# The first batch of an attention and expert kernel, written out by itself: keys ahead of queries, in pairs, partly with fp32 operands

## The chip, the core and the metric

The kernel runs on one core of one Trainium2 chip. The metric is the device time of one execution in microseconds (us); three runs of the kernel before are given, and one further execution that the profiler recorded. TensorE (PE) does matrix products, VectorE (DVE) and ScalarE (ACT) elementwise work, GpSimd (POOL) spreads rows over partitions, and SyncE (SP) issues the DMAs. Each engine works through its own queue in order and waits on semaphores of the others.

## What is computed

```python
x = L0_attn_x                       # (8, 1024, 256), 8 batches
x = _layernorm(x + _L0_attn_ref(x, L0_attn_Wqkv, L0_attn_bqkv, L0_attn_Wln, L0_attn_bln), axis=-1)
x = _layernorm(x + _L0_ffn_ref(x, L0_ffn_expert_sel, L0_ffn_keys, L0_ffn_values), axis=-1)

# attention, with b batches, N = 1024 rows, C = 256
qkv = x @ Wqkv + bqkv
q, k, v = jnp.split(qkv, 3, axis=2)
q = q - q.mean(axis=2, keepdims=True)
k = k - k.mean(axis=2, keepdims=True)
q2 = q * q
k2 = k * k
q2 = q2 / (q2.sum(axis=2, keepdims=True) + EPS_SUM)
q2 = _l2norm(q2, axis=-1)
k2 = k2 / (k2.sum(axis=2, keepdims=True) + EPS_SUM)
k2 = _l2norm(k2, axis=-2)
kv = jnp.einsum('bnc,bnd->bcd', k2, v)
t2 = jnp.einsum('bnc,bcd->bnd', q2, kv) / math.sqrt(N)
return (v + t2) @ Wln + bln

# 16 experts of width 128
sel = jax.nn.sigmoid(jnp.einsum('bsd,ed->bse', input_tensor, expert_sel))
scores = jax.nn.relu(jnp.einsum('bsd,edh->bseh', input_tensor, keys))
out = jnp.einsum('bseh,ehv,bse->bsv', scores, values, sel)
```

## The kernel before

A batch has 8 tiles of 128 rows (T = 8), in two groups of four. Nearly every fp32 product is made of three fp32r products: each operand is split into a high part, which ScalarE copies in fp32r, and a low part, which VectorE (in one place GpSimd) makes as the difference. `product` (L966 to L975) issues high times high, high times low and low times high.

The stages of layer 1 carry short names. QK projects one tile to q and k (512 columns). GG adds one tile's part to G = x^T k2, which stands for k2^T x. KS sums the columns of k2 and k2^2 over all tiles with products of 2 columns. KV makes G times Wv Wln. QT transposes two tiles of q2, Y makes the attention output of one tile from x times Wv Wln and q2 times kv, XT transposes the normalised tile x1, LG makes the expert logits of one group. ZA and ZN are the end of layer 2. Layer 2 runs in steps: in step s of an iteration TensorE makes the up product of one expert for one group, VectorE gates it (relu times sel, L950), ScalarE and VectorE split the gated tile (`gated_h`, `gated_l`), and TensorE makes the down product one step later. An iteration has 32 steps; the table LOOP says which stages of the batch ahead are done in which step, so that layer 1 of batch b + 1 lies under layer 2 of batch b.

Layer 1 of the first batch has nothing to lie under. The kernel before runs an iteration number -1 for it with the same step function, without the expert products, after the table FIRST: steps 7 to 14 with one QK each and GG behind, then KS, KV, QT 0 and 1, Y 0 to 3, XT 0 to 3 and LG 0. Tiles 4 to 7 of QT and Y stay for iteration 0. Odd tiles of QK use other buffers (`up_bank` and `gated` instead of `qk_bank` and `qk`), so names of layer 2 turn up in rows of layer 1. `wqk_split_hi` and `wqk_split_lo` centre and split the projection weights, `centre_qk_bias`, `spread_bv`, `make_wvl` (L981 to L992) and `wvl_esel_hi`, `wvl_esel_lo` prepare bias, Wv Wln and the selection weights. GpSimd makes the low part of the second half of xT and adds the fourth powers of k (`k4_total`, L474).

The expert weights come in eight pieces, alternating keys and values. `weights_hi` and `weights_lo` (L927) split them at the steps of PIECE_STEPS and PIECE_LO_STEPS, three in iteration -1 and five in iteration 0. The function table for the sigmoid is loaded at step 20 of iteration -1 (L651), before the logits are copied.

## Time and profile before

| | |
|---|---|
| runs | 1044.91, 1043.44, 1042.62 us, median 1043.44 |
| profiled execution, its own time | 1041.46 us |
| its span, first to last instruction | 1039.6 us |
| busy: TensorE, VectorE, ScalarE, GpSimd | 1008.7, 796.1, 509.2, 219.9 us |
| mean granted TensorE clock | 0.995 of full |
| chain that ended last | TensorE 95%, VectorE 3%, ScalarE 1% |

The busy times are those of the instructions' own records, which overlap a little on each engine: a product of 256 columns has a record of 0.28 us, and the next starts 0.11 to 0.12 us after it. How long a row of instructions takes is therefore best read from the chain that ended last, where each piece lasts until the next one begins. The idle time of an engine counts only where another waits for it.

### The profile page before, as it was taken

To read this page: it belongs to the slowest core of one execution; us is meant where nothing else is said; L and a number is where in the kernel's file an instruction comes from. 1 tells how busy PE (TensorE), PEld (TensorE's weight loads), DVE (VectorE), ACT (ScalarE), POOL (GpSimd) and SP (SyncE) were. 2 spreads that over 40 slices of the span, in tenths; PEclk is the share of its full clock that TensorE was granted. 3 is DMA by queue.
4 is the path that set the end of the run, shared out by engine and by line. 5 is a ranking of instruction groups with operands and counts; after the bars stand their busy time and mean duration, and the time that the engine had idled before them with its cause. 6 is when DMAs were issued, how large, how long until landed. Compare 5 with 4: busy or idle time off the path is not lost.

```text
span 1039.6 us, 18353 instructions
## 1 busy us (share of the span) xinstructions
PE 1008.7 (97%) x6636; PEld 914.7 (88%) x6636; DVE 796.1 (77%) x1818; ACT 509.2 (49%) x1192; POOL 219.9 (21%) x273
## 2 busy tenths in 40 slices
PE   5789999999999999999999999999999999999997
PEld 4669899988999899998999989999899988999986
DVE  6888886878868787778877779687886878867565
ACT  6555643465434653356534565255653465434332
POOL 2121122211221121221212211221122211221221
PEclk9999999999999999999999999999999999999999
DMA  5032000200011000110001100011000200000000
GB/s 180 21 117 68 2 22 1 83 21 3 21 43 62 2 2 21 43 61 2 2 21 43 61 3 21 1 57 48 2 22 1 83 21 3 22 2 21 2 21 21
DMA packets 12122, 32.59 MB, mean 31 GB/s; under 512 B 1792, under 2 KB 2048, under 8 KB 12032
## 3 DMA queue, kind: packets, MB, share of 16 engines
q1 hardware_dynamic: 12032, 31.42, 8.9%
q8 instruction: 53, 0.87, 0.3%
q14 instruction: 37, 0.30, 0.1%
HBM read 22.50 MB, written 8.39 MB: 30 GB/s over the span
## 4 chain that ended last, share of the span: by engine, by line
PE 95%; DVE 3%; ACT 1%; issue 0%; DMA 0%; ACTq 0%
PE down_bank L974 34%; PE up_bank L974 34%; PE ring_bank L974 10%; PE qk_bank L974 8%; PE g_bank L974 4%; PE ring_bank L1073 1%; PE ring_bank L1057 1%; PE ring_bank L1083 1%; PE ring_bank L1082 1%; PE ring_bank L1038 1%; DMA x<-in_wqk 0%; DVE keys_l L927 0%; DVE k_l L870 0%; DVE qk L738 0%; DVE q L922 0%
## 5 line engine op out<-in xcount | busy, mean ns | idle before, releaser
L504 ACT ACTIVATE gated_h<-gated 128x512 fp32r<-128x512 f32 x256 | 161.4, 631 | 403.4 <-DVE gated L950 403.4
L490 POOL PARTITION_BROADCAST sel_all<-sel_rows x240 | 196.8, 820 | 710.6 <-DVE gated L950 709.9
L974 PE MATMUL down_bank<-vals_h,gated_h 128*128 128x256 f32 x1024 | 292.0, 285 | 0.9 <-DVE gated_l L956 0.8
L974 PE MATMUL down_bank<-vals_l,gated_h 128*128 128x256 f32 x1024 | 285.3, 279 | 0.0
L974 PE MATMUL down_bank<-vals_h,gated_l 128*128 128x256 f32 x1024 | 285.3, 279 | 0.0
L950 DVE SCALAR_TENSOR_TENSOR gated<-up_bank,sel_all 128x512 f32<-128x512 f32 x256 | 176.0, 688 | 63.2 <-PE up_bank L974 62.0
L956 DVE TENSOR_TENSOR gated_l<-gated,gated_h 128x512 fp32r<-128x512 f32 x256 | 173.3, 677 | 43.5 <-ACT gated_h L504 42.5
L974 PE MATMUL up_bank<-x1T_h,keys_l 128*128 128x512 f32 x512 | 202.3, 395 | 0.0
L974 PE MATMUL up_bank<-x1T_l,keys_h 128*128 128x512 f32 x512 | 202.0, 394 | 0.0
L974 PE MATMUL up_bank<-x1T_h,keys_h 128*128 128x512 f32 x512 | 201.3, 393 | 0.0
L974 PEld LDWEIGHTS down_bank<-vals_h,gated_h 128*128 128x128 f32 x1024 | 193.2, 189 | 9.1 <-DVE gated_l L956 3.2
L974 PEld LDWEIGHTS down_bank<-vals_l,gated_h 128*128 128x128 f32 x1024 | 192.9, 188 | 4.6
L974 PEld LDWEIGHTS down_bank<-vals_h,gated_l 128*128 128x128 f32 x1024 | 192.7, 188 | 0.0
L974 PEld LDWEIGHTS up_bank<-x1T_h,keys_l 128*128 128x128 f32 x512 | 96.7, 189 | 20.4
L974 PEld LDWEIGHTS up_bank<-x1T_l,keys_h 128*128 128x128 f32 x512 | 96.9, 189 | 11.5
L974 PEld LDWEIGHTS up_bank<-x1T_h,keys_h 128*128 128x128 f32 x512 | 96.7, 189 | 11.1
L738 DVE TENSOR_TENSOR qk<-qk_bank,qk_bias 128x512 f32<-128x512 f32 x60 | 41.3, 689 | 36.6 <-PE qk_bank L974 36.6
L974 PE MATMUL qk_bank<-wqk_h,xT_h 128*128 128x512 f32 x120 | 50.0, 417 | 9.8 <-DVE xT_l L718 9.8
L751 DVE TENSOR_TENSOR y<-ring_bank,x_raw 128x256 f32<-128x256 f32 x64 | 27.0, 423 | 31.3 <-PE ring_bank L974 31.3
L974 PE MATMUL qk_bank<-wqk_h,xT_l 128*128 128x512 f32 x120 | 48.3, 402 | 0.0
L974 PE MATMUL qk_bank<-wqk_l,xT_h 128*128 128x512 f32 x120 | 48.3, 402 | 0.0
L504 ACT ACTIVATE k_h<-k,k_scale 128x256 fp32r<-128x256 f32 x64 | 32.6, 509 | 28.1 <-DVE k_scale L785 27.5
(156 smaller groups left out, 1655.1 us busy)
## 6 DMA issues: line engine op xcount, KB each, us to landing
xT_raw<-in_xT SPq DMA_DIRECT2D x16, 512.0 KB, 3.7
x_raw<-in_x SPq DMA_DIRECT2D x16, 512.0 KB, 4.5
out<-z SPq DMA_DIRECT2D x32, 256.0 KB, 2.3
w_room<-in_keys SPq DMA_DIRECT2D x4, 512.0 KB, 4.7
z<-in_values SPq DMA_DIRECT2D x4, 512.0 KB, 3.8
sel_rows<-sel SPq DMA_DIRECT2D x64, 8.0 KB
x<-in_wqk SPq DMA_DIRECT2D x1, 512.0 KB, 3.5
sel_all<-in_b_qk SPq DMA_DIRECT2D x1, 256.0 KB, 5.6
```

What stands on the lines that cost most here:

```text
L490: nc.gpsimd.partition_broadcast(sel_all[:, e % 2], row, P).then_inc(sel_spread, 1)
L504: return nc.scalar.activation(dst, src, ACT.Copy, **kw)
L738: V.tensor_tensor(qk_of(it, t)[:], qk_bank_of(it, t)[:], qk_bias[:], ALU.add).then_inc(qk_biased, 1)
L751: V.tensor_tensor(y[:, a % 2], ring_of(it, s, "Y", a)[:, 0:C], x_raw[:, a], ALU.add).then_inc(y_added, 1)
L950: V.scalar_tensor_tensor(out=gated[:], in0=up_bank[s % 2][:], scalar=0.0, in1=sel_all[:, s % 2], op0=ALU.max, op1=ALU.mult).then_inc(gate_ ...
L956: V.tensor_tensor(gated_l[:, s % 2], gated[:], gated_h[:, s % 2].bitcast(F32), ALU.subtract).then_inc(gated_lo, 1)
L974: last = mm(dst, lhs, rhs, start=start and i == 0, stop=stop and i == n - 1, **kw)
L1038: last = mm(bk[:, j:j + 2], total[:, m * P:(m + 1) * P], ones[:, 0:2], start=True, stop=True)
L1057: last = nc.tensor.transpose(bk[:, j:j + P], q2[:, 2 * a + i, m * P:(m + 1) * P], ident[:])
L1073: last = nc.tensor.transpose(bk[:, m * P:(m + 1) * P], x1[:, a, m * P:(m + 1) * P], ident[:])
L1082: mm(bk[:], esel_hl[:, m], x1T_h[:, a, m], start=(m == 0), stop=False)
L1083: last = mm(bk[:], esel_h[:, m], x1T_l[:, a, m], start=False, stop=(m == M - 1))
```

## The change

The iteration -1 is gone. Each engine has a function `first_batch`, which it runs before the loop and in which its part of the first batch is written out in its own order.

- TensorE projects the keys alone, two tiles at a time into one bank (`qk0`, `keys0`), with the bias as a last product of a row of ones and a split bias (`bias_hl`); queries follow in pairs later (`queries0`), pairs 2 and 3 only around the transposes of x1. Squares are taken by ScalarE straight from the bank.
- G, KV and the q part of Y are plain fp32 products (`g0`, `kv0`, `y0_of_q`): x, the normalised k2, G and kv are not split for them. The x part of Y (`y0_of_x`) stays in three fp32r products and is issued ahead of the column sums and KV.
- The sums over tiles of k2 and k2^2 are kept for even and odd tiles apart, both on VectorE, and the column sums have eight products instead of four. GpSimd has no elementwise work any more.
- wqk is loaded and treated in its key half and its query half, and the first batch's xT in four quarters.
- Two weight pieces instead of three are split before the loop, six in the loop. In iteration 0 the stages QT 2, QT 3 and Y 4 come one step later (FIRST_PLAN).
- In all batches q_sum and the floor that was made from it are gone; a constant floor Q_FLOOR^2 is applied to the sum of fourth powers (`lift_q4`), and ScalarE's two other activations on q keep or drop their accumulated sum accordingly.

The core of the diff, first the tables and the loads, then ScalarE, VectorE and TensorE. Functions named there and not shown do what their line in the list above says, with one wait for what they read and one for the buffer that they write.

```diff
+FIRST_PLAN = {
+    0: [], 1: [("QT", 2)], 2: [("QT", 3)], 3: [("Y", 4)], 4: [("Y", 5)], 5: [("Y", 6), ("XT", 4)],
+    6: [("Y", 7), ("XT", 5)]}
+FIRST = dict(LOOP, plan={**LOOP["plan"], **FIRST_PLAN})
...
-SIGMOID_STEP = 20
-PIECE_STEPS = ((-1, 9), (-1, 17), (-1, 20), (0, 0), (0, 2), (0, 3), (0, 5), (0, 7))
-PIECE_LO_STEPS = ((-1, 10), (-1, 18), (-1, 21), (0, 1), (0, 3), (0, 4), (0, 6), (0, 8))
-PIECE_LOADS = ((-1, 11), (-1, 19), (-1, 24), (0, 1), (0, 3), (0, 4))
+EARLY_PIECES = 2
+PIECE_STEPS = ((0, 0), (0, 1), (0, 4), (0, 6), (0, 8), (0, 10))
+PIECE_LO_STEPS = ((0, 1), (0, 2), (0, 5), (0, 7), (0, 9), (0, 11))
+PIECE_LOADS = ((0, 1), (0, 2), (0, 4), (0, 6), (0, 8))
+QUARTER = GN // 2
...
+            def load_xT0(p):
+                cols = slice((p % 2) * QUARTER, (p % 2 + 1) * QUARTER)
+                at_least(sp, xT0_lo, p - 1)
+                sp.dma_start(xT_raw[:, :, cols], xT[0, :, p // 2, :, cols]).then_inc(xT0_in[p], 16)
+            sp.dma_start(wqk_raw[:, :, 1], wqk[:, :, 1]).then_inc(w_k_in, 16)
+            load_xT0(0)
             sp.dma_start(bqk_raw, b_qk.partition_broadcast(P)).then_inc(bias_in, 16)
+            load_xT0(1)
...
+            for p in (2, 3):
+                load_xT0(p)
+            sp.dma_start(x_raw[:, GT:T], x_dram[0, :, GT:T]).then_inc(x_in[1], 16)
             for i in range(2):
                 load_piece(i)
+            sp.wait_ge(piece_lo, 1)
+            load_piece(2)
+            move_rows(0, 0, 0)
             def step(it, s):
...
+                        nc.scalar.activation(k0[:, i], k0_bank(p)[:, i * C:(i + 1) * C], square,
+                                             accum_out=k_sum[:, i:i + 1]).then_inc(k0_squared, 1)
+                def k_fourths(p):
+                    act.wait_ge(k0_normed, p + 1)
+                    at_least(act, k0_fourth_summed, p - 1)
...
+                        t = 2 * p + i
+                        nc.scalar.activation(q2[:, t], q0_bank(p)[:, i * C:(i + 1) * C],
+                                             square).then_inc(q0_squared, 1)
+                    for i in range(2):
+                        t = 2 * p + i
+                        act.wait_ge(q0_squared, t + 1)
+                        nc.scalar.activation(q0_bank(p)[:, i * C:(i + 1) * C], q2[:, t], square,
+                                             accum_out=q4_sum[:, t:t + 1]).then_inc(q0_fourth, 1)
...
+                act.wait_ge(constants_set, 2)
+                nc.scalar.activation(table_ahead[:, 0:1], eps_ln[:], sqrt)
+                w_hi(1, 1)
+                xT_pair_hi(0)
+                act.wait_ge(qk_bias_set, 2)
+                copy(bias_hl, qk_bias[:], scale=2.0 / P).then_inc(bias_hi, 1)
+                xT_pair_hi(1)
+                k_squares(0)
+                w_hi(0, 2)
+                k_fourths(0)
+                k_squares(1)
+                xT_pair_hi(2)
+                k_fourths(1)
+                k_squares(2)
+                xT_pair_hi(3)
+                act.wait_ge(wvl_made, 1)
+                copy(wvl_h[:].rearrange("p m c -> p (m c)"), down_bank[0][:]).then_inc(wvl_hi, 1)
+                copy(wvl_f.rearrange("p m c -> p (m c)"), down_bank[0][:]).then_inc(wvl_copied, 1)
+                k_fourths(2)
+                k_squares(3)
+                k_fourths(3)
+                q_squares(0)
+                act.wait_ge(g0_made, T)
+                copy(gated[:], g_bank[:]).then_inc(g0_copied, 1)
+                q_squares(1)
+                act.wait_ge(cols0_copied, 1)
+                nc.scalar.activation(col_norm[:], col_sums[:, 0:M], sqrt).then_inc(cols0_rooted, 1)
+                act.wait_ge(q0_lifted, 1)
+                nc.scalar.activation(q_root[:, 0:GT], q4_lifted[:, 0:GT], sqrt).then_inc(q0_rooted, 1)
+                act.wait_ge(constants_set, 5)
+                act.wait_ge(small_in, 64)
+                copy(esel_hl[:, :, 0:E], esel_raw[:])
+                copy(esel_h[:, :, 0:E], esel_raw[:]).then_inc(esel_hi, 1)
+                for p in range(2):
+                    act.wait_ge(q0_transposed, p + 1)
+                    copy(qT0[p].rearrange("p i m n -> p (i m n)"), q0T_bank(p)[:]).then_inc(q0_copied, 1)
+                weights_hi(0)
+                for p in range(2):
+                    for a in (2 * p, 2 * p + 1):
+                        act.wait_ge(y_aggregated, tile(0, a))
+                        nc.scalar.activation(y_std[:, a % 2:a % 2 + 1], y_mv[:, a % 2, 1:2], sqrt,
+                                             bias=eps_ln[:]).then_inc(y_rooted, 1)
+                    if p == 0:
+                        for m in range(M):
+                            act.wait_ge(kv0_scaled, m + 1)
+                            copy(kvw_h[:, m], kvw0[:, m]).then_inc(kv_hi, 1)
+                    for a in (2 * p, 2 * p + 1):
+                        act.wait_ge(x1_transposed, tile(0, a))
+                        copy(x1T_h[:, 0, :, a * P:(a + 1) * P],
+                             y0_bank(a)[:, 0:C].rearrange("p (m n) -> p m n", m=M)).then_inc(x1T_hi, 1)
+                q_squares(2)
+                q_squares(3)
+                act.wait_ge(q0_lifted, 2)
+                nc.scalar.activation(q_root[:, GT:T], q4_lifted[:, GT:T], sqrt).then_inc(q0_rooted, 1)
+                nc.scalar.activation(table_ahead[:, 1:2], eps_ln[:], ACT.Sigmoid)
+                act.wait_ge(logits_made, 1)
+                copy(sel[:], logits0_bank[LOW:LOW + E, :]).then_inc(logits_low, 1)
...
+                def k_normalised(p):
+                    dve.wait_ge(k0_squared, 2 * p + 2)
+                    V.tensor_scalar(k_sum_eps[:], k_sum[:], EPS_SUM, None, ALU.add).then_inc(k0_eps, 1)
+                    dve.wait_ge(k0_eps, p + 1)
+                    V.reciprocal(k_scale[:], k_sum_eps[:]).then_inc(k0_scaled, 1)
+                    dve.wait_ge(k0_scaled, p + 1)
+                    at_least(dve, g0_made, 2 * (p - 1))
+                    at_least(dve, k0_fourth, p - 1)
+                    V.tensor_tensor(k0_normal[p % 2], k0[:], k_scale[:].unsqueeze(2).broadcast_to((P, 2, C)),
+                                    ALU.mult).then_inc(k0_normed, 1)
...
+                w_centre(1, 1, w_k_in)
+                w_lo(1, 1)
+                xT_pair_lo(0)
+                qk_bias_centred()
+                bias_rows()
+                xT_pair_lo(1)
+                spread_bv()
+                k_normalised(0)
+                w_centre(0, 2, w_q_in)
+                xT_pair_lo(2)
+                k_normalised(1)
+                k_total(1)
+                w_lo(0, 2)
+                xT_pair_lo(3)
+                k_normalised(2)
+                k_fourth_total(1)
+                k_total(2)
...
+                k_normalised(3)
+                k_fourth_total(2)
+                k_total(3)
+                k_fourth_total(3)
...
+                x_bias(0)
...
+                q_lift(0)
+                q_scales(0)
...
+                for m in range(M):
...
+                x_bias(1)
+                for a in range(2):
+                    y_add(a)
+                for a in range(2):
+                    y_finish(a)
+                for a in range(2):
+                    y_add(2 + a)
+                    x1T_low(a)
+                for a in range(2):
+                    y_finish(2 + a)
+                weights_lo(0)
+                for a in range(2):
+                    x1T_low(2 + a)
...
+                q_lift(1)
+                dve.wait_ge(logits_low, 1)
+                V.tensor_tensor(sel[:], logits0_bank[0:E, :], sel[:], ALU.add).then_inc(logits_summed, 1)
+                q_scales(1)
+                for i in range(2):
+                    x_bias(2 + i)
+                weights_lo(1)
...
+            def first_batch():
+                def qk0(bank, p, a):
+                    cols = slice(a * C, (a + 1) * C)
+                    for i in range(2):
+                        h, n = divmod(2 * p + i, GT)
+                        product(bank[:, i * C:(i + 1) * C],
+                                [(both(xT_h, xT_l, ALL, h, m, slice(n * P, (n + 1) * P)),
+                                  both(wqk_h, wqk_l, ALL, m, cols)) for m in range(M)],
+                                start=i == 0, stop=False, skip_group_check=True)
+                    pe.wait_ge(constants_set, 5)
+                    pe.wait_ge(bias_lo, 1)
+                    return mm(bank[:], ones_r, bias_hl[:, cols].unsqueeze(1).broadcast_to((P, 2, C)),
+                              start=False, stop=True, skip_group_check=True)
...
+                def g0(p):
+                    pe.wait_ge(k0_normed, p + 1)
+                    pe.wait_ge(x_in[p // 2], 16)
+                    for i in range(2):
+                        a = 2 * p + i
+                        for m in range(M):
+                            last = mm(g_bank[:, m * C:(m + 1) * C], x_raw[:, a, m * P:(m + 1) * P],
+                                      k0_normal[p % 2][:, i], start=(a == 0 and m == 0), stop=(a == T - 1),
+                                      skip_group_check=True)
...
+                            last = nc.tensor.transpose(q0T_bank(p)[:, j:j + P], q2[:, 2 * p + i, m * P:(m + 1) * P],
+                                                       ident[:])
+                    last.then_inc(q0_transposed, 1)
+                def y0_of_q(a):
+                    pe.wait_ge(q0_copied, a // 2 + 1)
+                    pe.wait_ge(kv0_scaled, M)
...
+                keys0(0)
+                keys0(1)
+                make_wvl()
+                g0(0)
+                keys0(2)
+                g0(1)
+                keys0(3)
+                g0(2)
+                make_bvl()
+                queries0(0)
+                g0(3)
+                queries0(1)
+                y0_of_x(0)
+                y0_of_x(1)
+                column_sums()
+                kv0()
+                y0_of_x(2)
+                y0_of_x(3)
+                q0_transpose(0)
+                q0_transpose(1)
+                for a in range(GT):
+                    y0_of_q(a)
+                queries0(2)
+                for a in range(GT):
+                    x1_transpose(a)
+                    if a == 1:
+                        queries0(3)
+                logits0()
```

On VectorE, at the start, the kernel before has this (names without buffer numbers; `x` is the room in which wqk is staged):

```order
L670 TENSOR_REDUCE minus_mean<-x 128x4
L672 TENSOR_SCALAR minus_mean<-minus_mean 128x4
L676 SCALAR_TENSOR_TENSOR wqk_l<-x,minus_mean,wqk_h 128x256 x4
L718 TENSOR_TENSOR xT_l<-xT_raw,xT_h 128x1024
L682 TENSOR_REDUCE bias_mean<-sel_all 128x2
L684 TENSOR_SCALAR bias_mean<-bias_mean 128x2
L687 TENSOR_SCALAR qk_bias<-sel_all,bias_mean 128x256 x2
L696 TENSOR_SCALAR y<-ones,bv_col 128x128 x2
```

The changed kernel has this in the same place:

```order
L975 TENSOR_REDUCE minus_mean<-x 128x2
L977 TENSOR_SCALAR minus_mean<-minus_mean 128x2
L986 SCALAR_TENSOR_TENSOR wqk_l<-x,minus_mean,wqk_h 128x256 x2
L994 TENSOR_TENSOR xT_l<-xT_raw,xT_h 128x2x256
L999 TENSOR_REDUCE bias_mean<-sel_all 128x2
L1001 TENSOR_SCALAR bias_mean<-bias_mean 128x2
L1004 TENSOR_SCALAR qk_bias<-sel_all,bias_mean 128x256 x2
L1012 SCALAR_TENSOR_TENSOR x1T_h<-qk_bias,x1T_h 64x512
L994 TENSOR_TENSOR xT_l<-xT_raw,xT_h 128x2x256
L1020 TENSOR_SCALAR y<-ones,bv_col 128x128 x2
```

The same steps stand in the same order at half the width, with the bias rows (L1012) and a second quarter of xT put in.

On ScalarE, at the end of the prologue, up to the first split of a gated tile, before:

```order
L504 ACTIVATE x1T_h<-ring_bank 128x2x128 x2
L651 ACT_TABLE_LOAD
L651 ACTIVATE table_ahead<-eps_ln 128x1
L504 ACTIVATE keys_h<-w_room 128x1024
L504 ACTIVATE sel<-ring_bank 16x512
L573 ACTIVATE sel<-sel 16x512
L504 ACTIVATE gated_h<-gated 128x512
```

And in the changed kernel, from the last squares of the queries (`q` and `q_sum` are order's short names for q2 and q4_sum):

```order
L662 ACTIVATE g_bank,q_sum<-q 128x256 x2
L657 ACTIVATE q<-down_bank 128x256 x2
L662 ACTIVATE down_bank,q_sum<-q 128x256 x2
L718 ACTIVATE q_root<-q_lifted 128x4
L719 ACT_TABLE_LOAD
L719 ACTIVATE table_ahead<-eps_ln 128x1
L494 ACTIVATE sel<-down_bank 16x512
L723 ACTIVATE sel<-sel 16x512
L494 ACTIVATE vals_h<-z 128x1024
L494 ACTIVATE gated_h<-gated 128x512
```

Two pairs of queries and a root now stand ahead of the table load, and the weight piece stands behind the sigmoid.

On VectorE, between the sum of the logits and the first two gates, before:

```order
L909 TENSOR_TENSOR sel<-ring_bank,sel 16x512
L927 TENSOR_TENSOR keys_l<-w_room,keys_h 128x1024
L922 TENSOR_SCALAR q<-q,q_scale 128x256 x4
L950 SCALAR_TENSOR_TENSOR gated<-up_bank,sel_all 128x512
L956 TENSOR_TENSOR gated_l<-gated,gated_h 128x512
```

And in the changed kernel:

```order
L1165 TENSOR_TENSOR sel<-down_bank,sel 16x512
L1053 RECIPROCAL q_scale<-q_root 128x4
L1057 TENSOR_SCALAR q<-q,q_scale 128x256 x4
L1064 TENSOR_TENSOR x_raw<-x_raw,out_bias 128x512 x2
L947 TENSOR_TENSOR vals_l<-z,vals_h 128x1024
L960 SCALAR_TENSOR_TENSOR gated<-up_bank,sel_all 128x512
L966 TENSOR_TENSOR gated_l<-gated,gated_h 128x512
```

A reciprocal and two additions of the bias to x have come in ahead of the first gate.

## Rows read from the trace of the kernel before

**Rows 1.** Stretches: start:end, us, busy time of each engine, clock, DMA share, GB/s.

```profile
0.00:9.80 9.80, 0.00 (x0) 0.03 (x1) 4.43 (x8) 4.76 (x8) 0.93 (x8) 1.00 0.81 257
9.80:64.59 54.79, 41.46 (x216) 33.44 (x216) 44.67 (x113) 32.30 (x96) 11.55 (x12) 0.94 0.19 62
64.59:100.00 35.41, 35.41 (x238) 32.46 (x238) 30.71 (x63) 20.61 (x43) 7.36 (x9) 1.00 0.35 117
```

**Rows 2.** Waits of TensorE, whole span: us in total, times, longest.

```profile
PE g_bank L974 <- DVE k_l L870: 6.3, 4, 2.6
...
PE down_bank L974 <- DVE gated_l L956: 0.8, 1, 0.8
```

**Rows 3.** Chain that ended last, the start: start us, us, what.

```profile
0.72 3.54 DMA x<-in_wqk
...
4.29 1.23 DVE minus_mean L670
...
5.75 1.70 ACT wqk_h L510 x4
...
8.43 1.24 DVE xT_l L718
...
9.80 2.90 PE qk_bank L974 x6
```

**Rows 4.** DMA issues by line: count, KB each, median us from issue to landing.

```profile
out<-z SPq DMA_DIRECT2D x32, 256.0 KB, 2.3
...
ident<-in_ident SPq DMA_DIRECT2D x1, 64.0 KB, 5.1
```

**Rows 5.** Timeline, the prologue: start us, us, engine, line, operation.

```profile
5.81 0.85 SPq L426 DMA_DIRECT2D ident<-in_ident  x1
...
39.78 0.99 PE L1038 MATMUL ring_bank<-ones,k_total 128*128 128x2 f32 x8
```

**Rows 6.** Chain that ended last, pieces used as prices.

```profile
14.11 1.73 PE down_bank L987 x8
...
16.70 1.42 PE qk_bank L974 x6
...
26.15 1.13 DVE keys_l L927
27.29 0.60 DVE qk L738
...
34.69 0.40 ACT qk L554 x2
...
64.18 0.44 PE ring_bank L1057 x4
...
69.10 1.36 PE down_bank L974 x12
```

**Rows 7.** Timeline, end of the prologue.

```profile
56.05 1.28 ACT L651 ACT_TABLE_LOAD   x1
...
57.34 0.20 ACT L651 ACTIVATE table_ahead<-eps_ln 128x1 f32<-128x1 f32 x1
...
58.51 0.59 ACT L504 ACTIVATE sel<-ring_bank 16x512 f32<-16x512 f32 x1
...
59.13 0.68 DVE L909 TENSOR_TENSOR sel<-ring_bank,sel 16x512 f32<-16x512 f32 x1 [2.04 <-ACT sel L504]
...
60.87 1.67 DVE L922 TENSOR_SCALAR q<-q,q_scale 128x256 f32<-128x256 f32 x4
...
62.47 0.67 DVE L950 SCALAR_TENSOR_TENSOR gated<-up_bank,sel_all 128x512 f32<-128x512 f32 x1
...
64.59 0.39 PE L974 MATMUL down_bank<-vals_h,gated_h 128*128 128x256 f32 x1
```

**Rows 8.** Timeline, step 2 of the loop.

```profile
70.41 0.66 DVE L956 TENSOR_TENSOR gated_l<-gated,gated_h 128x512 fp32r<-128x512 f32 x1
...
71.67 0.28 PE L974 MATMUL down_bank<-vals_h,gated_h 128*128 128x256 f32 x1
```

647 lines of the change are left out of this document (388 added, 259 removed), and 5 rows, old and new, of the table plan.

## The prediction

> **What bounds the kernel now.** Read the stretches first [rows 1]. In the first 9.80 us TensorE does nothing, in the next 54.79 us it is busy for 41.46, and from 64.59 us, where the first product with the values of an expert starts, it is busy without a gap (35.41 of 35.41 us, and so on to the tail). From there the kernel is a TensorE queue of fixed length, and the change leaves that part's products as they are. So only one number matters: the moment at which that first down product starts, plus what is left of TensorE's work behind it. The waits [rows 2] say what holds it before: the key products of G wait 6.3 us in all for the low parts that VectorE makes, and the first down product waits for VectorE too (0.8 us). The prologue is therefore a relay of VectorE, ScalarE and TensorE, with TensorE filling what it can. The sum is made against the profiled execution: span 1039.6 us, its own time 1041.46 us; the median of the runs is 1043.44 us, 2.0 above it, and I forecast the median by taking the difference off it.
>
> **The start.** The chain [rows 3] is: 3.54 us for the 512 KB of wqk, then a reduction of 1.23, ScalarE's four high parts 1.70, xT high, xT low 1.24, first product at 9.80. The change loads and treats only the key half of wqk and a quarter of xT first. 256 KB land in 2.3 us for an output pair, against 3.54 for the 512 KB [rows 3, 4]; I take 2.5, landing at 3.2 (bounds 3.0 and 4.3). Everything behind is half as wide: reduction 0.7, scaling 0.2, two high parts 0.9, xT high 0.6, xT low 0.7 make the first product start at 6.4, which is 3.4 earlier. The first products still run at the half clock: six of 512 columns took 2.90 us right after the idle start and 1.42 later [rows 3, 6]. Half the columns twice over is the same work, so the first pair ends near 9.5; its closing bias product waits for the bias chain on VectorE, which ends near 9.1.
>
> **The key rounds.** VectorE's queue now holds the spread of b_v ahead of the first k_normalised, and that needs the small loads. The last of them was issued at 5.81 and landed 5.1 later, at 10.9 [rows 4, 5]; 256 KB less stand ahead of it, at 257 GB/s [rows 1] that is 1.0 us, so about 10.1. Behind it, in handed-over steps, priced at 0.60 to 0.7 for 512 columns on VectorE, 0.40 for a square of 256 on ScalarE [rows 6]: spread 0.5, normalising pair 0 1.1 (to 11.65), centring the query half 0.8 (12.4), its high parts 0.9 and the fourth powers 0.5 on ScalarE (13.8), squares of pair 1 0.85 (14.65), xT high and low of quarter 2 1.35 (16.0). TensorE meanwhile did pair 1, wvl and G of pair 0, to 14.9, and waits 1.1. Then pair 2 to 17.8, its squares to 18.6, xT high and low of quarter 3 to 20.0.
>
> **TensorE's stretch.** From 20.0 it has its own queue to do, and VectorE keeps ahead of it: four wvl products in fp32 took 1.73 us, 0.43 each, against three fp32r products of 256 columns at 0.113 each (twelve in 1.36) [rows 6]. So fp32 costs TensorE 0.09 us per product more, and saves the splitting into high and low parts on the two engines that are waited for. The list is keys pair 3 1.6, G 1.7, bvl 0.85, queries 1.6, G 1.7, queries 1.6, two x parts of Y 1.4, and eight column sums. Eight records, which are four such products, took 0.99 [rows 5], so eight take 1.7 to 2.0. Sum 12.3, to 32.3. KV in fp32 and two more x parts (3.1) lie beside VectorE's work on the column sums, bias on x, q scales and kv: 0.3, 0.6, 0.7 with two square roots of ScalarE, 1.5, 1.6, to 37.1. That is when the q part of Y can start. Four q parts in fp32 take 3.45, queries pair 2 1.6. VectorE's add, statistics and normalisation of each of tiles 0 to 3 are three instructions of 256 columns, the price of a square (0.40), with short ones between, 1.5 a tile; in one queue with two low parts of x1T they end near 45.6, transposing and ScalarE's last high part at 46.4.
>
> **The tail of the prologue,** where the change puts work that was not there before. ScalarE now squares queries of pairs 2 and 3 (eight at 0.40, 3.3), takes a root (0.35 with VectorE's lift), loads the sigmoid table (1.28) and only then copies the logits (0.60) [rows 6, 7]. The table load lay beside the logits products before and costs its full length now. That makes 52.0, the sum on VectorE (0.68) 52.7. Behind that sum VectorE has four scalings of q (0.2 for the reciprocal, 1.6 as in the row of four), two biases on x (1.2), and a weight piece (1.13) before the first gate: 56.8. GpSimd's spread of sel lies beside it. Before, one piece and the four scalings stood there. From gate to down product 62.47 to 64.59, 2.1 us [rows 7]. The down product thus starts at 58.9; some fifteen hand-overs of 0.03 to 0.05 that I rounded away add 0.4: **59.3, against 64.59, a gain of 5.3**.
>
> What is given back: at that moment QT 3 was already done before and is not now, four transposes, 0.4 [rows 6]. TensorE will have stood for about 6 us between the second up product and this down product with only a few transposes in it. The clock was at its lower level after 9.8 idle us until the first six products had run, which cost 2.90 - 1.42 = 1.5 [rows 3, 6]; I take 1.5 again (bounds 0 and 2.0). Six weight pieces are split within the first batch's loop instead of five, at steps 1, 2, 5, 7, 9, 11 instead of 1, 3, 4, 6, 8. A piece is 1.13 of VectorE. The tightest place that I saw is step 2, where gated_l (70.41, 0.66 long) ended 0.6 ahead of its product at 71.67 [rows 8]; the Y that made it tight moves to step 3 with the extra piece, others have 1 to 2.9, and only step 12 gets a piece that is not compensated. I count 0.3. Sum: -5.3 + 0.4 + 1.5 + 0.3 = -3.1. The removal of q_sum, its floor and its maximum, and of the accumulate for every tile lies on engines that nobody waits for later, nothing. 1043.44 - 3.1 = **1040.4 us**.
>
> **The rivals.**
> A, the clock does not fall or the wait is short, 0.18: the 1.5 is not paid, -4.6, 1038.8. For it: the transposes in the gap; against: the gap is about 6 us long, and the only gap of that size before the loop was followed by the low clock.
> B, the start does not come early, 0.20: four loads are cut into runs half as long. If these halves landed at half the rate, about 1 MB would need 3.7 us more before the query half and quarter 2 arrive, and VectorE waits for these from 11.6 on. The down product starts at 62.6 and the sum is +0.2: 1043.6, no change. For it: the DMA engines are at 0.81 of their time in the first stretch [rows 1]; against, the packets are no smaller than 1 KB.
> C, slower, 0.09: the six pieces in the first twelve steps. VectorE is busy 30.71 of 35.41 us there [rows 1]. With one more piece and Y shifted, each piece that is not covered stops TensorE for 1.13 at the down product of that step. It decides from the third on, since 3 x 1.13 = 3.4 is more than the 3.1 won; with five of six, 5.6 less the 0.3 counted, the sum is +2.2: 1045.6. Against: the slack of 1 to 2.9 at the other steps.
> D, the table load holds ScalarE longer than its row, 0.05: a second 1.28 on the path, -1.8, 1041.6. In the trace the load runs 56.05 to 57.33 and the next activation starts at 57.34 [rows 7], which speaks against it.
> The Trainium skill, "ScalarE: Activation LUTs", section "What ACT_TABLE_LOAD costs", puts a drain of about 1380 ns beside the load of 1283 ns; the load agrees with the row, the drain is not seen in it. By that rule the time would be 1041.8 us, since the load is now on the path; by the row it is 1040.4.
> E, more is won, 0.08: the relay rows are shorter than handed-over ones wherever two steps follow on one engine (0.60 instead of 0.69), over some thirty such steps 2.5 more, 1037.9.
> The forecast itself has 0.40.
>
> **How the numbers follow.** About 0.2%, 2.1 us, is what a measurement of this kernel can tell from no change. The forecast lies 1.0 beyond that, and its own spread (w_k landing 3.0 to 4.3, column sums 1.7 to 2.0, clock 0 to 2.0) is about 2 either side: 0.30 of its 0.40 is faster, 0.10 the same. A and E are faster (0.26), with 0.05 of B: 0.61. Same: 0.10, 0.14 of B, 0.04 of D: 0.28. Slower: C, 0.01 of B and 0.01 of D: 0.11. The range takes in E, A and B and leaves out C and the far end of E: 1036.3 to 1044.9.
>
> **What would show it.** First product at 6.4 (wrong if after 8: rival B), fourth key pair at about 20, then TensorE gapless for 12 us; q part of Y at 37; VectorE behind ScalarE's table load and not the logits products as what releases sel; first down product at 59.3; its twelve matmuls at 0.21 apart if the clock is low, 0.113 if not (A); no wait of TensorE on gated_l afterwards (C). The prediction is wrong in its main step if the down product starts before 57 or after 61.5.

## The result, and the profile after

The kernel after takes **1053.9 us** (median; five runs lie from 1052.6 to 1054.2, and a sixth, of 1446.85 at a granted clock of 0.654, is left out), the kernel before 1044.2 (six runs, 1042.6 to 1047.1). The ratio is 1.0083, with a 95% interval of 1.0066 to 1.0101: slower by 0.8%, 9.7 us, where the forecast was 1040.4 and the range ended at 1044.9. The profiled execution took 1054.15 us, its span is 1052.4.

The first lines of the page after (us, share of the span, count):

```profile
span 1052.4 us, 18293 instructions
...
PE 1028.3 (98%) x6672; PEld 934.5 (89%) x6672; DVE 785.5 (75%) x1782; ACT 498.2 (47%) x1117; POOL 211.7 (20%) x266
```

TensorE is busy for 98% of the span, before for 97%. But that is 1028.3 us with 6672 product records, and the kernel before, with the same loop, is busy for 1008.7 with 6636. The stretches, to hold against [rows 1] (start:end, us, busy time with counts, clock, DMA share, GB/s):

```profile
core 0: us, PE busy (x) PEld busy (x) DVE busy (x) ACT busy (x) POOL busy (x), PEclk, DMA share, GB/s
0.00:9.80 9.80, 2.58 (x12) 2.61 (x12) 3.66 (x9) 2.91 (x5) 1.33 (x10) 1.00 0.69 191
9.80:62.81 53.01, 43.83 (x238) 37.89 (x238) 34.31 (x88) 26.85 (x78) 2.77 (x3) 0.92 0.25 78
62.81:100.00 37.19, 37.19 (x236) 34.10 (x237) 30.23 (x62) 20.51 (x42) 7.36 (x9) 0.94 0.32 108
...
300.00:900.00 600.00, 600.00 (x3926) 546.15 (x3925) 464.84 (x1059) 297.34 (x672) 125.80 (x153) 1.00 0.08 27
```

The first down product starts at 62.81, before at 64.59: the prologue is 1.8 us shorter, where 5.3 were forecast. From there to the end of the span are 989.6 us, before 975.1: **14.5 us more in the part that the prediction had taken as fixed.** TensorE hardly stands still there: its one listed wait is of 0.7 us, behind 1000 us, and the kernel before has one of 0.8 in the same place. In the 600 us from 300 to 900, in which TensorE is fully busy in both kernels, the view after counts 3926 products, and that of the kernel before 3975:

```profile
300.00:900.00 600.00, 600.00 (x3975) 546.48 (x3974) 471.67 (x1087) 304.63 (x721) 126.70 (x155) 1.00 0.08 28
```

So the same products follow each other more slowly. A stretch of the chain of work that ended last (start us, us, what), after, and then the same of the kernel before:

```profile
482.74 1.44 PE down_bank L1185 x12
484.18 1.40 PE up_bank L1185 x6
...
486.97 1.42 PE down_bank L1185 x12
488.39 1.40 PE up_bank L1185 x6
...
491.90 1.42 PE down_bank L1185 x12
```

```profile
481.27 1.38 PE down_bank L974 x12
482.65 1.37 PE up_bank L974 x6
...
489.60 1.42 PE down_bank L974 x12
491.01 1.40 PE up_bank L974 x6
...
493.81 1.38 PE down_bank L974 x12
495.19 1.37 PE up_bank L974 x6
```

Twelve down products take 1.42 to 1.44 here, and mostly 1.36 to 1.39, at times 1.42, before. Worked out from the starts of the products in the traces between 100 and 1000 us (means, gaps over 150 and 300 ns left out): one down product follows the other after 119.0 ns, before after 115.8, and one up product after 232.2, before after 230.4. In 256 steps of twelve and six that is 9.8 and 2.8 us, 12.6 of the 14.5. (By e1 below, whose 64 bytes alone take 11.9 off this part, 2.6 are left.) The rest was forecast in kind: 0.4 for QT 3 and 1.5 for the low clock, of which more below.

The waits of TensorE after, to hold against [rows 2]:

```profile
PE qk_bank L1185 <- DVE xT_l L994: 7.2, 1, 7.2
PE down_bank L1185 <- DVE gated_l L966: 5.1, 2, 4.4
PE down_bank L1314 <- DVE x1T_l L1087: 1.5, 1, 1.5
PE qk_bank L1206 <- DVE x1T_h L1012: 1.4, 1, 1.4
```

The waits of G's products for the low parts of the keys, 6.3 us before, are gone, as meant. The first down product waits 4.4 us for gated_l. The other 0.7 of that row, and the whole row of 0.8 in [rows 2], lie behind 1000 us: before, the first down product has no wait for gated_l in the list.

### The profile page after: what moved, and what is told of

The parts are those of the page before. It is cut to its first block, busy times and chain, and to the rows that moved or that the text cites. A ratio compares the mean times of both kernels' runs of the same rounds, so it can differ in the third digit from the quotient of the medians.

```text
span 1052.4 us, 18293 instructions
## 1 busy us (share of the span) xinstructions
PE 1028.3 (98%) x6672; PEld 934.5 (89%) x6672; DVE 785.5 (75%) x1782; ACT 498.2 (47%) x1117; POOL 211.7 (20%) x266
## 4 chain that ended last, share of the span: by engine, by line
PE 96%; DVE 2%; ACT 1%; DMA 1%; issue 0%; SPq 0%; DVEq 0%
PE down_bank L1185 35%; PE up_bank L1185 34%; PE ring_bank L1185 9%; PE qk_bank L1185 8%; PE g_bank L1185 4%; PE ring_bank L1418 1%; PE ring_bank L1402 1%; PE g_bank L1229 1%; PE ring_bank L1425 1%; PE ring_bank L1424 1%; DMA sel_all<-in_b_qk 1%; PE ring_bank L1387 1%; DVE q L1057 0%; PE down_bank L1239 0%; PE ring_bank L1298 0%
## 5 line engine op out<-in xcount | busy, mean ns | idle before, releaser
L1185 PE MATMUL down_bank<-vals_h,gated_l 128*128 128x256 f32 x1024 | 289.5, 283 | 0.0
L1185 PE MATMUL down_bank<-vals_l,gated_h 128*128 128x256 f32 x1024 | 289.3, 283 | 0.0
L1185 PEld LDWEIGHTS down_bank<-vals_h,gated_h 128*128 128x128 f32 x1024 | 194.5, 190 | 12.3 <-DVE gated_l L966 6.0
L1185 PE MATMUL up_bank<-x1T_h,keys_h 128*128 128x512 f32 x512 | 203.9, 398 | 0.0
L1185 PEld LDWEIGHTS down_bank<-vals_h,gated_l 128*128 128x128 f32 x1024 | 194.9, 190 | 0.0
L760 DVE TENSOR_TENSOR qk<-qk_bank,qk_bias 128x512 f32<-128x512 f32 x56 | 38.6, 689 | 36.4 <-PE qk_bank L1185 36.4
L1185 PE MATMUL qk_bank<-wqk_h,xT_h 128*128 128x512 f32 (+1 forms) x124 | 49.7, 400 | 7.2 <-DVE xT_l L994 7.2
L1185 PE MATMUL qk_bank<-wqk_h,xT_l 128*128 128x512 f32 (+1 forms) x124 | 48.2, 388 | 0.0
L1185 PE MATMUL qk_bank<-wqk_l,xT_h 128*128 128x512 f32 (+1 forms) x124 | 48.1, 388 | 0.0
L494 ACT ACTIVATE k_h<-k,k_scale 128x256 fp32r<-128x256 f32 x56 | 28.5, 510 | 25.0 <-DVE k_scale L812 24.4
```

Of the source, the lines that this page charges most:

```text
L494: return nc.scalar.activation(dst, src, ACT.Copy, **kw)
L760: V.tensor_tensor(qk[:], qk_bank[:], qk_bias[:], ALU.add).then_inc(qk_biased, 1)
L1185: last = mm(dst, lhs, rhs, start=start and i == 0, stop=stop and i == n - 1, **kw)
```

## The experiments

The question: what makes the loop's products slower, whose instructions the change leaves alone? Three things that a diff of the program's text doesn't show are different in the loop. The buffers behind q2 lie 64 bytes lower in each partition, since q_sum and q_floor (32 bytes each) are gone (theory ADDRESS). The two ring banks are exchanged (RING): thirteen uses of the ring in iteration -1 are gone, so that each later use falls on the other bank. And the loop starts at another moment, with other semaphore counts (PHASE).

**e1, the 64 bytes given back.**

```diff
+        room_a = sb("room_a", [P, T])
-        q4_sum, q_root, q_scale = (...)
+        q4_sum, q_root = sb("q4_sum", [P, T]), sb("q_root", [P, T])
+        room_b = sb("room_b", [P, T])
+        q_scale = sb("q_scale", [P, T])
```

> The kernel after with two unused buffers of 32 bytes a partition where q_sum and q_floor stood, so that every buffer behind q2 (x1T, gated_h, gated_l, k2_h, qT, kvw) has the address that it has in the kernel before. No instruction changes. Theory ADDRESS (the loop's products became slower because these operands moved down by 64 bytes): down products in the loop at 113 to 118 ns apart again instead of 120, twelve in 1.36 or 1.42 us, and the time falls by about 11.7 us, to 1042.2. Rival RING (the ring banks of the whole loop are exchanged, 0 for 1): no change, 1053.9. Rival PHASE (the loop follows from the moment at which the prologue hands over, the counts of semaphores or the place of the instructions): no change, 1053.9.

Measured: 1042.33 us (1040.9 to 1043.5), ratio to before 0.9984, interval 0.9969 to 1.0000. The same stretch and the same piece of the chain:

```profile
300.00:900.00 600.00, 600.00 (x3974) 546.34 (x3974) 470.62 (x1079) 301.01 (x680) 126.67 (x154) 1.00 0.08 28
```

```profile
480.37 1.37 PE up_bank L1188 x6
...
483.13 1.38 PE down_bank L1188 x12
484.51 1.37 PE up_bank L1188 x6
...
487.99 1.38 PE down_bank L1188 x12
489.37 1.37 PE up_bank L1188 x6
```

3974 products in 600 us, down products 115.7 ns apart; from the first down product to the end are 977.7 us, 11.9 less than after. Two unused buffers are worth 11.6 us.

**e2, the kernel before with q_sum and q_floor moved to the end of the buffers.**

```diff
-        q_sum, q4_sum, q_root, q_floor, q_scale = (...)
+        q4_sum, q_root, q_scale = (...)
...
+        q_sum, q_floor = sb("q_sum", [P, T]), sb("q_floor", [P, T])
```

> The kernel before with q_sum and q_floor moved to the end of the buffers, so that everything behind q2 moves down by 64 bytes, to the addresses of the kernel after. No instruction changes. ADDRESS: about 11.7 us slower, 1055.1, down products of twelve at 1.44 us all through the loop. RING and PHASE: no change, 1043.4 to 1044.2.

Measured: 1057.62, ratio 1.0124 (1.0092 to 1.0157); 3921 products in the 600 us, 119.0 ns. It is 2.5 slower than expected. In the profiled execution the old prologue itself ended late (first down product at 67.86, before at 64.59), for a reason that the run does not show. From there to the end are 987.0 us, 11.9 more than before.

**e3, the ring banks exchanged back** (`ring_bank = [...][::-1]`).

> The kernel after with the two ring banks exchanged, so that in the loop each ring use has the PSUM bank that it has in the kernel before. ADDRESS and PHASE: no change, 1053.9. RING: about 11.7 us faster, 1042.2.

Measured: 1054.51, ratio 1.0098 (1.0070 to 1.0126), 3926 products. RING falls. PHASE had fallen with e1 already: there the prologue and the queues are those of the kernel after, and the pace is the old one.

**e4, only q_floor moved away, 32 bytes.**

> The kernel before with only q_floor moved to the end, so that everything behind q_root moves down by 32 bytes. ADDRESS leaves open what this gives, since no trace shows an offset of 32: between no change (1043.4) and the whole loss (1055.1); what it gives tells whether the step that matters is 32 or 64 bytes. RING and PHASE: no change.

Measured: 1055.36, ratio 1.0098 (1.0061 to 1.0136), 118.2 ns. The prologue ended late here too (69.99), and from there to the end are 984.7 us, 9.6 more than before. So 32 bytes cost the loop nearly as much as 64, which cost it 11.9.

**e5, gated back in its place** (64 unused bytes ahead of sel, so that sel, gated and what lies behind them move up, and nothing ahead of them).

> The kernel after with 64 unused bytes ahead of sel: gated_h and gated_l are back at the addresses of the kernel before, x1T, k2_h, qT and kvw are not. If the loss is each product's own, by its own operand, the down products fall from about 119.1 to about 115.7 ns apart (4 x 9.6 ns a step, 256 steps: 9.8 us) while the up products stay at 232.2 (their 9.2 ns a step, 2.4 us, stay lost): 1044.1. If what matters is x1T or another buffer ahead of it: no change, 1053.9. If all must be moved together: something in between.

Measured: 1044.18, ratio 0.9990 (0.9976 to 1.0003), against 1044.1 expected; down products 115.7 ns apart, up products still 232.0. So the loss belongs to each kind of product by itself, and the down products have some four fifths of it: from the first of them to the end are 979.8 us, 9.8 less than after, where e1 saved 11.9.

**e6, all buffers moved by 64 bytes, the values and keys too** (64 unused bytes ahead of keys_h).

> The kernel after with 64 unused bytes ahead of the first buffer: every buffer moves up by 64 bytes, so gated and x1T have the addresses of the kernel before, and keys, values and wqk, read in the same products, are moved by as much. If the address of gated and x1T alone counts: the time of the kernel after with room, 1042.3. If what counts is how far the two operands of a product lie apart: no change, 1053.9.

Measured: 1053.63, ratio 1.0084 (1.0059 to 1.0110), 118.9 ns. Here gated_h has the very address that was fast in e1, and the loop is as slow as after. **So the address of gated does not decide alone: the pace of a down product depends on the addresses of both its operands**, gated, which stays in TensorE, and the values, which stream. That only the distance between the two counts fits this run well (down products, up products and products of G are at 118.9, 232.2 and 118.8 ns, as after to within 0.1), but the test that would show it, a fast layout moved as a whole, was not run, and the products of G speak against it as the only rule (below).

**e7 and e8, 96 and 128 unused bytes where q_sum stood.**

> The kernel after with 96 unused bytes where q_sum stood: gated, x1T and all behind q2 lie 32 bytes above their place in the kernel before. Offsets of gated_h within 128 bytes seen so far: 64 fast, 0 and 32 slow. If 64 alone is fast: 1053 to 1056, as at 32. If what is wanted is the upper half of 128 bytes: 1042.3.

> The kernel after with 128 unused bytes where q_sum stood: all behind q2 lies 64 bytes above its place in the kernel before and 128 above the kernel after. If the pattern repeats every 128 bytes: as the kernel after, 1053.9. If it repeats at 64 bytes or is a matter of this one address: 1042.3 or something else.

Measured: e7 1052.80, ratio 1.0076 (1.0049 to 1.0102), 118.2 ns; e8 1052.57, ratio 1.0079 (1.0052 to 1.0105), 118.8 ns. For the down products only the distance of before is fast among five (0, 32, 64, 96 and 128 bytes).

**e9, every kind of product at that distance within 128 bytes** (32 unused bytes ahead of x_raw, 64 ahead of x_h, 96 ahead of k2_h, kvw_h and x1, 64 ahead of qT_h).

> The kernel after with unused bytes at six places, so that in every fp32r product the operand that stays in TensorE and the one that streams lie 64 bytes apart within 128: gated against values and x1T against keys as in the kernel before, and now also xT against wqk and wvl, x against k2, gT against wvl, qT against kvw. No instruction changes. Reading of the runs so far (each kind of product is slow by itself unless its two operands lie 64 apart): the products of G fall from 118 to 115 ns (some 336 of them, 1 us), those of Y from 118 to 115.5 (768, 1.9 us), those of queries and keys from 233 to 230.5 (336, 0.8 us), down and up as with room for 64 bytes: 1042.3 - 3.7 = 1038.6. If the queue locks into the fast pace of 113.3 ns more often because the products ahead of it are fast too, the down products give up to 7 more: down to 1031. Rival (only down and up products are sensitive, the rest moved by chance): 1042.3.

Measured: 1049.74, ratio 1.0046 (1.0032 to 1.0060). A miss by 11 us on the wrong side: the down products were at 117.7 and the up products at 233.7. "64 within 128" was not the rule: counted within 256 bytes, gated now lies 192 from the values.

**The prologue.** Three runs on the kernel after with 64 bytes of room (e1 is the base, 1042.3, measured on another chip) took up the terms of the sum.

e10, the tail:

```diff
-  nc.scalar.activation(table_ahead[:, 1:2], eps_ln[:], ACT.Sigmoid)
   act.wait_ge(logits_made, 1)
   copy(sel[:], logits0_bank[LOW:LOW + E, :]).then_inc(logits_low, 1)
+  nc.scalar.activation(table_ahead[:, 1:2], eps_ln[:], ACT.Sigmoid)
...
   q_scales(1)
-  for i in range(2):
-      x_bias(2 + i)
-  weights_lo(1)
```

The piece comes behind the first gate, one bias addition behind the first gated_l, the other at step 3.

> The kernel after with 64 bytes of room, and the end of the prologue in another order: ScalarE copies the logits before it loads the sigmoid table, and VectorE does the two additions of the bias to x and the low part of the second weight piece behind the first gate instead of ahead of it. In the run with room the first gate started at 61.88, 5.3 after the sum of the logits, and the spread of the first row of sel had ended some 2.9 earlier. Theory TAIL (the first down product is late because of what VectorE has ahead of the gate, with ScalarE's table load in the path): the first down product 3 to 3.5 us earlier and the time down by about 3, to 1039.3, if the loop's first steps can take the 1.3 us of bias additions. Rival (the work comes back as waits of TensorE in the first steps): 1042.3.

Measured: **1038.36** (1037.3 to 1039.2), ratio 0.9933 (0.9913 to 0.9953). First down product at 59.45. The timeline (start us, us, engine line op out<-in, idle before):

```profile
52.80 0.59 ACT L495 ACTIVATE sel<-down_bank 16x512 f32<-16x512 f32 x1
...
53.41 1.28 ACT L722 ACT_TABLE_LOAD   x1
53.42 0.68 DVE L1170 TENSOR_TENSOR sel<-down_bank,sel 16x512 f32<-16x512 f32 x1 [0.88 <-ACT sel L495]
...
54.22 1.14 DVE L1069 TENSOR_SCALAR q<-q,q_scale 128x256 f32<-128x256 f32 x4
...
56.50 0.69 DVE L968 SCALAR_TENSOR_TENSOR gated<-up_bank,sel_all 128x512 f32<-128x512 f32 x1 [1.14 <-POOL sel_all L481]
57.11 1.22 DVE L948 TENSOR_TENSOR vals_l<-z,vals_h 128x1024 fp32r<-128x1024 f32 x1
...
59.45 0.39 PE L1187 MATMUL down_bank<-vals_h,gated_h 128*128 128x256 f32 x1 [2.76 <-DVE gated_l L976]
```

The copy lies ahead of the table load, VectorE's sum beside it, and the gate waits for the spread of sel and no longer for VectorE. The work put behind it did not come back as waits: from the first down product to the end are 976.0 us, with one wait for gated_l of 0.2 in the first steps. Not all of the 4.0 is the order of the tail. From the end of the column sums to the first down product are 24.0 us, in e1 and in the kernel after 26.8: that is 2.8. The part behind is 1.7 shorter than in e1 (977.7), with the clock at its full level there.

e11, the loads: the query half of wqk issued ahead of x, the four small loads last, and the spread of b_v behind the low part of xT's fourth quarter.

> The kernel after with 64 bytes of room, and the query half of wqk loaded fourth, the small loads last, and the spread of b_v three steps later in VectorE's queue. In the run with room VectorE stood for 1.84 us on the last small load before the spread and the first normalising (13.62), and TensorE then 2.16 at the third key pair. Theory LOADS: the third key pair starts at about 17.5 instead of 19.4, the column sums end about 1.9 earlier, the time falls by about 1.5 to 1040.8. Rival (with the clock still low at that time TensorE is the bound and the order of the loads is worth nothing): 1042.3.

Measured: 1040.50 (1039.2 to 1042.0), ratio 0.9954 (0.9938 to 0.9969). The third key pair starts at 17.39 (19.43 in e1), as expected. The column sums end at 34.12, 3.0 earlier than in e1 (37.08), but the profiled execution of e1 was its slowest; against the kernel after (35.96) it is 1.8. The edit changes VectorE's order as well as that of the loads, and the two were not taken apart.

e12, products of ones with ones that nobody reads, in the gaps of TensorE:

```diff
+NFILL = 14
...
+                for i in range(12):
+                    mm(ring_bank[0][:, 0:P], ones[:], ones[:], start=True, stop=True)
                 keys0(0)
...
+                if it == 0 and s == LAG:
+                    for i in range(NFILL):
+                        mm(qk_bank[:, 0:P], ones[:], ones[:], start=True, stop=True)
```

> The kernel after with 64 bytes of room, and products of ones with ones that nobody reads: twelve of 128x128 in fp32 ahead of the first key product, and fourteen ahead of the first down product, in the time in which TensorE has nothing to do. Theory CLOCK (the idle stretches cost the half clock for some 3 to 7 us after them): granted clock at full level from the first key product on and over the first down products, the first two key pairs 1.4 us each shorter (partly hidden behind VectorE), the first down and up products 1.4 and 1.2 instead of 2.9 and 2.3: 2.5 to 4 us less, 1039. Rival (these are hidden, or the fill holds up real products): 1042.3 or more.

Measured: 1040.12 (1039.6 to 1042.9), ratio 0.9953 (0.9936 to 0.9970). Granted clock around the first down products, of e1 and of this run:

```profile
65.00:70.00 5.00, 5.00 (x24) 4.44 (x24) 3.12 (x4) 2.08 (x4) 0.59 (x2) 0.62 0.60 197
```

```profile
65.00:70.00 5.00, 5.00 (x37) 4.59 (x36) 4.21 (x6) 2.06 (x3) 0.80 (x1) 1.00 0.37 127
```

At 0.62 the array ran mostly at its lower level, 1.2 GHz, behind a gap; with the gap filled it is at 1.00, 2.4 GHz. From the first down product to the end are 975.6 us instead of 977.7: the low clock costs 2.1 there, by one execution of each. In e10, where the gap is shorter, the clock is at 1.00 from 55 us on without a fill, and the same part takes 976.0. The fill ahead of the first key product brought little: its pair still waits for the bias rows (2.7 us ahead of the closing product), and the twelve products of the second pair take 2.50 us, so that most of them still ran at the low level.

**f1, all three together** (the fill ahead of the first down product with six products instead of fourteen).

> The kernel after with 64 bytes of room, the tail, the loads and the fill of the three runs before together (the fill ahead of the first down product with six products instead of fourteen, since the gap is shorter). If the gains add: 1042.3 - 4.0 - 1.8 - 2.2 = 1034.3. If they overlap (the clock in the tail is already full when the tail is short, and the fill at the start gives only what the loads then hide): 1036.5.

Measured: 1036.73 (1035.9 to 1037.6), ratio 0.9924 (0.9909 to 0.9939). Added up, the three gains would have given 1034.3, so they overlap by 2.4 us.

**f2, f3, f4: one kind of product at a time moved to 64 within 128, on the base of f1.** x_h and x_l (96 unused bytes ahead, 32 behind), xT (32 ahead, 96 behind), qT (64 and 64).

> The run with all three, and x_h and x_l moved so that they lie 64 from k2 (32 before); all else at the same distances. Theory ENTRY (a group of down products takes the pace at which the group ahead of it leaves the queue; behind the slow products of G none of 34 groups reached 113, behind up products 0.90, behind the q part of Y all): the groups behind G become fast, G itself 118 to 115: 336 x 3.3 ns = 1.1 us and 48 groups x 12 x 4.5 ns = 2.6 us, together 3.7 us less than the run with all three. If the pace is fixed by something else: 1.1 less, or nothing.

> The run with all three, and xT_h and xT_l moved so that they lie 64 from wqk and wvl (32 before). ENTRY: the x part of Y 118 to 115, the groups behind queries and keys (0.74 fast) all fast or all slow: between 3 less and 6 more than the run with all three. In the run in which every kind lay 64 apart, up products were at 233 and down products at 117.5 to 118; if that comes from xT, this run shows it (about 7 more).

> The run with all three, and qT_h and qT_l moved so that they lie 64 from kvw (0 before; at 0 every group of down products behind the q part of Y ran at 113). ENTRY with a slow group as the better lead: these 28 of 240 groups fall back to 118: 64 x 12 x 4.5 ns = 3.5 us more at most, less 0.8 for the products themselves. If each kind stands for itself: 0.8 less.

Measured: 1045.91, 1044.39 and 1044.24 (ratios 1.0014, 1.0002 to 1.0026; 0.9994, 0.9983 to 1.0005; 0.9996, 0.9985 to 1.0008), all 7.5 to 9.2 slower than f1, with down products at 117.6 or 117.7 ns. The three were badly cut: each has 128 unused bytes more ahead of x1T and gated as well. Either the products ahead of a group set its pace, or 128 bytes matter and the period is longer.

**g2, x alone**: x_h, x_l, qk and q2 moved up by 96 bytes and q4_sum, q_root, q_scale and q4_lifted put to the end, so that k2, x1T and gated stay where f1 has them. **g1**: 320 unused bytes where f1 has 64.

> The run with all three edits, x_h, x_l, qk and q2 moved up by 96 bytes and four small buffers moved to the end, so that G's operands lie 64 apart within 128 and k2, qT, x1T and gated stay exactly where they are. Theory PLACE (the 128 bytes by which gated and x1T stood higher made the three slow runs slow): the time of the run with all three, 1036.7, or 1 less; down products at 115.4 to 116.4. Theory ENTRY (another pace of G changes the groups behind it): as the run that changed x with the 128 bytes, 1045.9, down products at 117.5.

> The run with all three edits, with 320 unused bytes instead of 64 where q_sum stood: gated, x1T and all else behind q2 256 bytes higher, no distance changed modulo 256. PLACE with a period of 256 bytes: as the run with all three, 1036.7. PLACE with a longer period or none: slower, 1044 to 1046. ENTRY with a period of 128: 1036.7, as a move by 128 would then give too.

Measured: g2 **1035.90** (1035.4 to 1036.4), ratio 0.9919 (0.9897 to 0.9942), and g1 1035.95 (1035.9 to 1037.5), ratio 0.9924 (0.9897 to 0.9952), with down products at 115.8 and 115.7 ns. A move by 256 bytes changes nothing, one by 128 is what f2, f3 and f4 have in common, and they lost some 8 us. g2 is 0.8% faster than the kernel before. The 600 us stretch of f2 and of g2:

```profile
300.00:900.00 600.00, 600.00 (x3943) 544.51 (x3942) 467.35 (x1071) 299.83 (x679) 125.45 (x153) 1.00 0.08 27
```

```profile
300.00:900.00 600.00, 600.00 (x3985) 546.92 (x3984) 471.69 (x1083) 300.26 (x681) 126.67 (x154) 1.00 0.08 28
```

All runs on one scale, by the distance from vals_h to gated_h within 256 bytes (from the order and sizes of the buffers; the values stand at one address in all runs but e6):

| distance | runs | products in 300 to 900 us | down products apart, ns |
|---|---|---|---|
| 64 | before, e1, e5, e10, e11, e12, f1, g1, g2 | 3966 to 3985 | 115.7 to 115.9 |
| 0 | after, e2, e3, e6 | 3921 to 3926 | 118.9 to 119.0 |
| 32 | e4 | 3933 | 118.2 |
| 96 | e7 | 3932 | 118.2 |
| 128 | e8 | 3931 | 118.8 |
| 192 | e9, f2, f3, f4 | 3939 to 3951 | 117.6 to 117.7 |

**What stays open.** The means hide a pattern within a group of twelve. At 64, in 154 of 235 groups before and 164 in e1, the products end up 113 or 114 ns apart; some 25 of these groups do so from the first product, the others only after two to five steps of mostly 116 to 123 ns. The other groups stay at 117 to 119. At 0, 32, 96 and 128 no group ends at 113; at 0 most drift to 120 and stay there. Which way a group goes at 64 depends on more than its own operands: in f1, 1 of 34 groups behind products of G ended at 113, in g2, where x, qk and q2 had moved, 26 of 34, while behind queries and keys the number fell from 35 of 47 to 21, although the operands of these have the same addresses in both runs. By the means of these groups that is an estimated 0.8 us won and 0.4 lost, and it was not explained.

Nor is the distance of the two operands the whole rule for other kinds of product. The products of G have x_h and k2_h exactly 17728 bytes apart in e7, e9 and f2, and follow each other after 114.4, 118.0 and 118.2 ns (116.8 to 119.4 in all other runs). The up products are at 230.2 to 230.7 ns at the distances of before and of e8, at 232.0 to 232.6 at those of after and of e4, and at 233.5 to 233.7 in e7, e9 and f2 to f4. Whether the place of the operands by itself, the products ahead or something else is missing from the rule, why 64 is good for the down products, and what the best layout is, was not found.

## Why the prediction was wrong, step by step

- **"From there the kernel is a TensorE queue of fixed length, and the change leaves that part's products as they are."** This is the step that failed. The products are the same, their operands' addresses are not. Taking q_sum and its floor away was costed at nothing, on engines that nobody waits for, and nothing speaks against that for their instructions; their 64 bytes cost 11.6 us (e1; e2 from the other side). No rival had it. Without it the time is 1042.3 (e1), inside the range, but not for the forecast's reasons: the ratio 0.9984 can't be told from no change.
- **The start of the down products** is the second step that failed, by the prediction's own sign ("wrong in its main step if the down product starts before 57 or after 61.5"): it started at 62.81, a gain of 1.8 where 5.3 were summed. (That this product had waited 0.8 us for VectorE before was a misreading of [rows 2]; no term of the sum hangs on it.) The terms follow.
- **The loads.** The half of wqk landed at 4.00, forecast 3.2 (bounds 3.0 to 4.3): 256 KB took 3.28 us from their issue, hardly less than the 3.54 of 512 KB before [rows 3]. The 2.5 had followed the 2.3 of an output pair [rows 4]. The bias rows landed 6.3 us after their issue and held the first pair's closing product until 11.52, where the pair had been expected to end near 9.5; the last small load came at 13.4, forecast 10.1. The chain and VectorE's queue after:

```profile
2.12 6.31 DMA sel_all<-in_b_qk
...
11.52 0.77 PE qk_bank L1206
12.29 2.86 PE up_bank L1185 x12
...
23.36 1.66 PE up_bank L1185 x12
...
34.27 1.69 PE down_bank L1258 x16
```

```profile
4.00 0.69 DVE L975 TENSOR_REDUCE minus_mean<-x 128x2 f32<-128x512 f32 x1 [4.00 <-DMA x<-in_wqk]
...
8.45 0.69 DVE L999 TENSOR_REDUCE bias_mean<-sel_all 128x2 f32<-128x512 f32 x1 [1.37 <-DMA sel_all<-in_b_qk]
...
13.42 0.48 DVE L1020 TENSOR_SCALAR y<-ones,bv_col 128x128 f32<-128x128 f32 x2 [1.32 <-DMA ident<-in_ident]
```

  The first product started at 7.2 (forecast 6.4), the fourth key pair at 23.36 (20.0), the column sums ended at 35.96 (32.3). Rival B, the start does not come early, had the sign and the size (3.7 us) and the wrong transfer: VectorE never waited for the query half of wqk, it waited for the bias rows (1.37 us) and the last small load (1.32). (The text of B also leaves out the 0.4 of hand-overs: 59.3 and 3.7 give 63.0 and a time of 1044.0, not 62.6 and 1043.6.) The first stretch moved 191 GB/s, before 257 [rows 1]. e11 puts 1.8 us on the order of the loads and of VectorE's steps behind them. The second pair also still ran at the low clock, 2.86 for its twelve products against 1.65 where it had risen (e1, e10, e11; e1 has the same loads, so this differs between executions).
- **TensorE's stretch of 12.3 us** from the fourth key pair on: 12.6, right. The column sums took 1.69, at the lower bound. **Y, the transposes and the logits**: q part of Y from 40.51 (37.1 and 3.4 of start), ScalarE's last high part of x1T ended at 50.2, 3.8 later than forecast. Right apart from the start.
- **The tail.** Sum of the logits ended at 56.2 (52.7), the gate began at 60.69 (56.8), the first down product at 62.81 (59.3): 3.5 late, no more than the column sums were. That the table load would lie on the path is right, and e10 shows what it and the work ahead of the gate were worth: 2.8 in the tail itself and 4.0 together with the clock behind it. One term in the tail was mis-sized (timeline of the end of the prologue):

```profile
53.36 1.28 ACT L719 ACT_TABLE_LOAD   x1
...
54.65 0.20 ACT L719 ACTIVATE table_ahead<-eps_ln 128x1 f32<-128x1 f32 x1
...
55.49 0.68 DVE L1165 TENSOR_TENSOR sel<-down_bank,sel 16x512 f32<-16x512 f32 x1 [2.39 <-ACT sel L494]
...
56.28 1.68 DVE L1057 TENSOR_SCALAR q<-q,q_scale 128x256 f32<-128x256 f32 x4
...
59.09 1.68 DVE L947 TENSOR_TENSOR vals_l<-z,vals_h 128x1024 fp32r<-128x1024 f32 x1
...
60.69 0.68 DVE L960 SCALAR_TENSOR_TENSOR gated<-up_bank,sel_all 128x512 f32<-128x512 f32 x1
...
62.81 0.58 PE L1185 MATMUL down_bank<-vals_h,gated_h 128*128 128x256 f32 x1 [4.36 <-DVE gated_l L966]
```

  The weight piece took 1.68 us, costed at 1.13, with GpSimd's spread of sel beside part of it. In e10 it took 1.22, also with a spread beside it, so that this is not shown as the reason; the four scalings, with no spread beside them in e10, took 1.14 there and 1.68 here.
- **Rival D** fell: the table load runs from 53.36 to 54.64 and the next activation starts at 54.65. The drain of about 1380 ns that the Trainium skill gives beside the load ("ScalarE: Activation LUTs", "What ACT_TABLE_LOAD costs") is not seen here either, with the load now on the path: 0.01 us lies between the load and the next activation.
- **The clock.** Rival A fell too: it does drop. Against e1 the cost is 2.1 by e12, 1.7 by e10 and 1.1 by f1, all three at the full level there, where 1.5 was taken and 2.0 was the upper bound.
- **Rival C**, the six pieces in the first steps, fell: between the first down product and 1000 us TensorE has no listed wait for gated_l, so that the 0.3 was not paid either. In e10, with two bias additions put there as well, there is one of 0.2.
- **Rival E**, more is won, fell with the start.
- The gain of the change at equal addresses is between nothing and 3 us (0.9969 to 1.0000). It can't be told more closely, since the runs of the kernel before (but for one of 1443.4) lie from 1041.2 to 1047.4: those with a mean granted clock of 0.994 or more below 1044, those with 0.991 or less above 1044.7. The kernel after with room has 1040.9 to 1043.5.

## What to carry to other kernels

A diff that removes or adds a buffer moves every buffer behind it. In a kernel that is bound by TensorE, compare the addresses of the operands of its busiest products before and after, and the start-to-start time of one kind of product in the steady state, before a cause is looked for in what the change meant to do. Give hot buffers fixed places of their own. And an experiment on addresses must hold all other addresses in place: f2 to f4 moved two things at once and first suggested a wrong cause.
